# Projection stages with feed-forward parts: the loop over batch elements written out, with normalisations of two elements among the products of the one between

## The chip, the cores and the metric

The kernel runs on one core of a Trainium2 chip. The metric is the device time of one execution in microseconds (us), taken over several executions. TensorE (PE in the rows) multiplies, VectorE is DVE, ScalarE is ACT, GpSimd is POOL, and SyncE (SP) issues nearly all transfers.

## The reference

Two transformer blocks, one behind the other, on x of 4 batch elements x 512 rows x 256 features, with a context of 4 x 1601 x 192. Block 0 has 16 heads of 64, block 1 has 16 heads of 16. Each block does, with `ln` a normalisation over the features:

```python
x = attn(ln(x), ln(x), Wq1, Wk1, Wv1, Wo1, bo1) + x      # self-attention
x = attn(ln(x), context, Wq2, Wk2, Wv2, Wo2, bo2) + x    # cross-attention
x = feed_forward(ln(x)) + x
```

The feed-forward of block 0 is `(a * gelu(gate)) @ Wf` with `a, gate = split(h @ Wp)` (1024 wide each). Block 1 has `gelu(h @ w1) @ w2`, 1024 wide, once between its self- and its cross-attention and once at the end.

## The kernel before

`build` (L1600) runs nine stages one after the other: projections p0, p1, p2, p3, p4 (`project_phase`, L169) and between them attentions a0 to a3. q, k, v and the attention's result o go through DRAM from stage to stage. Every fp32 operand of a large product is split into a high part (fp32r, written by ACT) and a low part (the rest, by DVE), and a product is three products (`product3`, L350): high x high, high x low, low x high. Everything is held feature-major: 128 features on the partitions, 512 rows of x as columns.

A projection stage works through the 4 batch elements. Its steps, as (kind, m), are written out in one list, `order`, which every engine walks through in a hardware loop (`Fori`, L457, L573, L654, L759); the last element is written out once more. The kinds are:

- after 0, after 1 (L505): the attention's output projection of the *next* element, each tile in a PSUM bank of its own (6 and 7); residual (L675): its sum with x_from into x
- mean, var, scale, shift (L513 to L523, L592 to L609, L685 to L716): one normalisation. TensorE forms the mean with a matrix of ones (L499), DVE centres (L689), ACT squares (L595), TensorE forms the variance (L499), DVE adds epsilon (L695) and takes reciprocals (L698), ACT the root into `dev` (L599), DVE scales (L703), ACT writes z_hi (L607) and DVE z_lo (L712). m = 0 is the normalisation ahead of the first products of the next element; m = 1 the one between feed-forward and attention of the present element
- gate 0 to 7 and gate_end (L524, L610, L717): the first feed-forward product, gelu, and the split into u_hi (L588) and u_lo (L670). In p2 a gate has two products (`a` and the gate); in p3 and p4 one
- out 0, out 1 (L535, L733): the second feed-forward product, added to x
- context (L622, L729): the high and the low part of the context, in p1 and p3
- q, k, v (L539, L626, L631, L738): the projections for the next attention. q and k leave as two stores each from a ring of 4 (L402), v as one (L437) from v_sb, which has `VPL` slots: 4 where there is a context and a feed-forward (p3), otherwise 2 (p2)

p2 is projection and geglu feed-forward of block 0 with q, k, v of block 1's self-attention; p3 projection, feed-forward and q, k, v for block 1's cross-attention; p4 projection and feed-forward, whose x is the output. In p2 and p3 the order is such that of the next element only projection, residual and normalisation 0 stand behind the outputs, among q, k and v. In p4 nothing but after 1 stands behind the outputs before the norm.

The order around the change in p2 (L213), and the four DVE banks and one to four ACT banks that it uses (L487 to L494, NAB = 2 in stages with `after`):

```python
order = (gates + [("after", 0)] + outs + [("mean", 1), ("swap_x", 0), ("var", 1), ("after", 1),
                         ("scale", 1), ("shift", 1), ("residual", 0)] + qs[:1] + [("mean", 0)] + qs[1:]
         + ks[:1] + [("var", 0)] + ks[1:] + vs[:2] + [("scale", 0), ("shift", 0)] + vs[2:])
```

Weights come in pieces of up to 128 x 1024 words. Each lands in one of a few rooms (xc, sq, gate and so on, L336), is split (L651, L756; L753 for the lower 64 rows of the context weights), and the whole of them is split before the first residual (L652, L757). x has one buffer, so the store of x (L417) must be read out before the next residual (L679).

Of the kernel before, what the change touches and what calls it, by code (L numbers as in the profile page):

```python
# [16 lines left out]
ALU = mybir.AluOpType  # L17
# [68 lines left out]
def words(ap):  # L86

    return ap.bitcast(F32) if ap.dtype == F32R else ap


class Program:
# [27 lines left out]
    def sem(self, name):  # L119

        handle = self.phase_sems.enter_context(self.nc.semaphore(name))
        self.handles.append(handle)
        return handle
# [45 lines left out]
def project_phase(pr, name, after=None, ff=None, attn=None, x_in=None, x_out=None):  # L169
# [106 lines left out]
    with ExitStack() as st:  # L276
# [382 lines left out]
        def _(dve):  # L659
# [99 lines left out]
            with dve.Fori(0, B - 1, 1) as b:  # L759
                element(b, order)  # L760
            element(B - 1, last_order)


def attend_narrow(pr, name, a):
# [835 lines left out]
def build(nc, ins, out):  # L1600
    with ExitStack() as keep:
        pr = Program(nc, ins, out, keep)
        w0, w1 = "L0_xattn_", "L1_xattn_"
        setup_phase(pr)
        project_phase(pr, "p0", x_in=ins["x"],
                      attn=(SELF0, w0 + "g1", w0 + "b1", w0 + "Wq1", w0 + "Wk1", w0 + "Wv1"))
        attend_wide(pr, "a0", SELF0)
        project_phase(pr, "p1", x_in=ins["x"], x_out=pr.x, after=(SELF0, w0 + "Wo1", w0 + "bo1"),
                      attn=(CROSS0, w0 + "g2", w0 + "b2", w0 + "Wq2", w0 + "Wk2", w0 + "Wv2"))
        attend_wide(pr, "a1", CROSS0)  # L1610
        project_phase(pr, "p2", x_in=pr.x, x_out=pr.x, after=(CROSS0, w0 + "Wo2", w0 + "bo2"),
                      ff=("geglu", w0 + "g3", w0 + "b3", w0 + "Wp", w0 + "bp", w0 + "Wf", w0 + "bf"),
                      attn=(SELF1, w1 + "n1_g", w1 + "n1_b", w1 + "sq_w", w1 + "sk_w", w1 + "sv_w"))
        attend_narrow(pr, "a2", SELF1)
        project_phase(pr, "p3", x_in=pr.x, x_out=pr.x, after=(SELF1, w1 + "so_w", w1 + "so_b"),
                      ff=("gelu", w1 + "n2_g", w1 + "n2_b", w1 + "f1_w1", w1 + "f1_b1", w1 + "f1_w2", w1 + "f1_b2"),
                      attn=(CROSS1, w1 + "n3_g", w1 + "n3_b", w1 + "cq_w", w1 + "ck_w", w1 + "cv_w"))
        attend_narrow(pr, "a3", CROSS1)
        project_phase(pr, "p4", x_in=pr.x, x_out=out, after=(CROSS1, w1 + "co_w", w1 + "co_b"),
                      ff=("gelu", w1 + "n4_g", w1 + "n4_b", w1 + "f2_w1", w1 + "f2_b1", w1 + "f2_w2", w1 + "f2_b2"))  # L1620


# [45 lines left out]
```

## Time and profile before

| | us |
|---|---|
| median of 3 runs | 3775.29 |
| lowest, highest | 3765.72, 3777.51 |
| profiled execution, its own time | 3764.11 |
| span of the profile | 3762.3 |
| mean granted TensorE clock | 0.928 |
| MB moved by the transfers | 588 |
| stage p2: first load issued, last product | 2044.3, 2380.6 |
| stage p3 | 2619.1, 2938.1 |
| stage p4 | 3552.1, 3758.5 |

A busy share is time in which an engine had an instruction under way, over the span. A duration of a TensorE product overlaps the next one, so its pace is read from starts, not from durations. PEclk is the granted TensorE clock as a share of 2.4 GHz. A wait names what ended it, not what caused it. The three stages are 861.8 us of the span when the transfers between their last product and the next stage are left out.

### The profile page before, as it was taken

To read this page: it belongs to the slowest core of one execution; us is meant where nothing else is said; L and a number is where in the kernel's file an instruction comes from. 1 tells how busy PE (TensorE), PEld (TensorE's weight loads), DVE (VectorE), ACT (ScalarE), POOL (GpSimd) and SP (SyncE) were. 2 spreads that over 40 slices of the span, in tenths; PEclk is the share of its full clock that TensorE was granted. 3 is DMA by queue.
4 is the path that set the end of the run, shared out by engine and by line. 5 is a ranking of instruction groups with operands and counts; after the bars stand their busy time and mean duration, and the time that the engine had idled before them with its cause. 6 is when DMAs were issued, how large, how long until landed. Compare 5 with 4: busy or idle time off the path is not lost. (4 is left out here: it accounts for less than half of the span.)

```text
span 3762.3 us, 50843 instructions
## 1 busy us (share of the span) xinstructions
PE 3270.4 (87%) x17084; PEld 1864.8 (50%) x17084; DVE 2258.7 (60%) x4090; ACT 1815.4 (48%) x3349; POOL 1081.9 (29%) x538
## 2 busy tenths in 40 slices
PE   7969995999799999999996778597778599999776
PEld 5734443878544444444443566332566444444254
DVE  4447774334366666666663444496444499999333
ACT  4425552445244444444443333286343188888633
POOL 0036670000077777777775000022000000000000
PEclk9979997999799999999998999698899599999888
DMA  5888866999966666666652331344453523322210
GB/s 204 282 194 225 228 165 244 326 333 302 255 144 148 148 149 148 149 148 148 148 141 103 133 113 39 96 132 147 162 179 102 151 83 106 103 98 88 82 71 34
DMA packets 364807, 588.00 MB, mean 156 GB/s; under 512 B 47042, under 2 KB 200226, under 8 KB 363470
## 3 DMA queue, kind: packets, MB, share of 16 engines
q1 hardware_dynamic: 359478, 582.00, 52.6%
q10 hardware_dynamic: 5112, 3.25, 0.5%
q8 instruction: 118, 1.93, 0.2%
q14 instruction: 99, 0.81, 0.1%
HBM read 341.51 MB, written 240.88 MB: 155 GB/s over the span
## 5 line engine op out<-in xcount | busy, mean ns | idle before, releaser
L1506 ACT ACTIVATE a_prob<-a_ring 128x512 f32<-128x512 f32 (+1 forms) x1088 | 575.4, 601 | 656.3 <-PE a_ring L1411 584.4
L1532 DVE TENSOR_REDUCE a_blk_max<-a_ring 128x1 f32<-128x402 f32 x1024 | 519.5, 567 | 327.6 <-PE a_ring L1395 327.5
L1092 ACT ACTIVATE a_prob<-a_ring 128x512 f32<-128x512 f32 (+1 forms) x1088 | 582.3, 605 | 97.0 <-PE a_ring L1012 93.2
L1361 POOL TENSOR_TENSOR a_prob_sum<-a_prob,a_prob_sum 128x1024 f32<-128x1024 f32 x256 | 599.4, 2379 | 2.7 <-ACT a_prob L1506 2.7
L1137 DVE TENSOR_REDUCE a_blk_max<-a_ring 128x1 f32<-128x402 f32 x1024 | 506.7, 567 | 63.6 <-PE a_ring L999 56.9
L1433 PE MATMUL a_pv<-a_prob,a_v 128*64 128x512 f32 (+1 forms) x2176 | 534.8, 610 | 0.0
L1410 PE MATMUL a_ring<-a_q_stack,a_k_stack 128*128 128x512 f32 (+1 forms) x1088 | 463.9, 426 | 13.8 <-DMA a_q_second<-maxima 12.7
L1411 PE MATMUL a_ring<-a_q_second,a_k_second 65*128 65x512 f32 (+1 forms) x1088 | 435.6, 400 | 0.0
L1361 POOL TENSOR_TENSOR a_prob_sum<-a_prob 128x1024 f32<-128x1024 f32 x128 | 302.0, 2370 | 412.1 <-DVE a_chunk_sum L1563 244.2
L1030 PE MATMUL a_pv<-a_prob,a_v 128*32 128x256 f32 (+2 forms) x4096 | 340.7, 406 | 13.7 <-ACT a_prob L1092 7.8
L742 DVE TENSOR_TENSOR p_split_lo<-p_ps,p_split_hi 128x512 fp32r<-128x512 f32 (+2 forms) x280 | 171.2, 621 | 298.0 <-ACT p_split_hi L630 297.3
L999 PE MATMUL a_ring<-a_k_stack,a_q_stack 63*128 63x402 f32 (+1 forms) x1280 | 284.8, 425 | 65.2 <-DMA a_q_stack<-a_prob 61.1
L1410 PEld LDWEIGHTS a_ring<-a_q_stack,a_k_stack 128*128 128x128 f32 (+1 forms) x1088 | 204.8, 188 | 169.1 <-issue 116.6
L1395 PE MATMUL a_ring<-a_k_stack,a_q_stack 64*128 64x402 f32 (+1 forms) x1280 | 245.5, 428 | 48.0 <-DMA a_q_stack<-q_hi_cross 21.8
L1012 PE MATMUL a_ring<-a_q_stack,a_k_stack 64*128 64x512 f32 (+1 forms) x1088 | 279.8, 484 | 1.0
L630 ACT CAST p_split_hi<-p_ps 128x512 fp32r<-128x512 f32 (+2 forms) x280 | 147.4, 533 | 273.5 <-PE p_ps L355 113.3
L1395 PEld LDWEIGHTS a_ring<-a_k_stack,a_q_stack 64*128 64x128 f32 x1280 | 113.2, 191 | 285.9 <-issue 181.6
L1433 PEld LDWEIGHTS a_pv<-a_prob,a_v 128*64 128x64 f32 (+1 forms) x2176 | 131.7, 137 | 243.8 <-issue 150.8
L999 PEld LDWEIGHTS a_ring<-a_k_stack,a_q_stack 63*128 63x128 f32 x1280 | 146.4, 196 | 164.5 <-issue 68.2
L1411 PEld LDWEIGHTS a_ring<-a_q_second,a_k_second 65*128 65x128 f32 (+1 forms) x1088 | 206.3, 190 | 38.2
L1532 DVE TENSOR_REDUCE a_row_max<-a_ring 128x1 f32<-128x512 f32 x256 | 158.7, 683 | 96.8 <-PE a_ring L1395 96.8
L1012 PEld LDWEIGHTS a_ring<-a_q_stack,a_k_stack 64*128 64x128 f32 (+1 forms) x1088 | 110.7, 182 | 209.9 <-ACT a_prob L1092 81.3
(252 smaller groups left out, 4666.2 us busy)
## 6 DMA issues: line engine op xcount, KB each, us to landing
a_k_stack<-k_hi_cross SPq DMA_DIRECT2D x96, 400.5 KB, 4.6
a_v<-v_cross SPq DMA_DIRECT2D x48, 768.0 KB
a_k_stack<-k_lo_cross SPq DMA_DIRECT2D x80, 400.5 KB, 6.0
a_k_second<-k_hi_cross SPq DMA_DIRECT2D x32, 801.0 KB, 12.7
v_cross<-p_v_sb SPq DMA_DIRECT2D x48, 512.0 KB, 4.1
k_hi_cross<-p_split_hi SPq DMA_DIRECT2D x120, 200.0 KB, 3.2
k_lo_cross<-p_split_lo SPq DMA_DIRECT2D x120, 200.0 KB, 3.2
a_q_stack<-q_hi_self SPq DMA_DIRECT2D x64, 256.0 KB, 4.2
```

The source lines that it names most:

```text
L999: nc.tensor.matmul(ring[:, n % BANKS, 0:a.blk], qst[i % SLOTS][rows, j, t * P:(t + 1) * P], kst[i % SLOTS][rows, j, at:at + a.blk], start= ...
L1012: nc.tensor.matmul(ring[0:keys, n % BANKS, :], kst[i % SLOTS][rows, j, ch * P:ch * P + keys], qst[i % SLOTS][rows, j, :], start=True, stop ...
L1030: last = nc.tensor.matmul(pv[32 * h:32 * h + 32, cols], v[i % SLOTS][0:keys, ch, 32 * h:32 * h + 32], prob[0:keys, tau % RC, h, cols], sta ...
L1092: nc.scalar.activation(prob[0:keys, tau % RC, m, :], ring[0:keys, score_place(e) % BANKS, :], ACT.Exp, scale=a.scale).then_inc(exp_done, 1)
L1137: nc.vector.reduce_max(dst, ring[:, item_place(g) % BANKS, 0:a.blk], AX.X).then_inc(item_read, 1)
L1361: nc.gpsimd.tensor_tensor(prob_sum[:, h], prob_of(i * NCP + cp, h), other, ALU.add)\
L1395: nc.tensor.matmul(ring[:, max_bank(g), 0:a.blk], qst[i % SLOTS][rows, h, t * P:(t + 1) * P], kst[i % SLOTS][rows, h, at:at + a.blk], star ...
L1410: nc.tensor.matmul(out, kst[s][:, h, k0:k0 + keys], qst[s][:, h, :], start=True, stop=False)
L1411: nc.tensor.matmul(out, k2[s][:, h, k0:k0 + keys], q2[s][:, h, :], start=False, stop=True)\
L1433: last = nc.tensor.matmul(pv[64 * h:64 * h + 64, :], v[i % SLOTS][0:keys, ch, 64 * h:64 * h + 64], prob_of(w, h)[0:keys, ch % 2, :], start ...
L1506: nc.scalar.activation(prob_of(w, h)[0:keys, ch % 2, :], ring[0:keys, score_bank(e), :], ACT.Exp, scale=a.scale).then_inc(exp_done, 1)
L1532: nc.vector.reduce_max(dst, ring[:, max_bank(g), 0:a.blk], AX.X).then_inc(item_read, 1)
```

## The change

p2, p3 and p4 are built by a new function, `feed_phase`; `project_phase` stays for p0 and p1. Its instructions are those of `project_phase`, with these differences:

- no hardware loop: one list, `steps`, of (kind, m, element) over all four elements
- x has two buffers, chosen by the element's parity; `dev` is gone and the root goes back into `var`; xc, sq and var stay single
- DVE's tiles use PSUM banks 0 to 3 in turn, projections too, ACT's tiles banks 4 to 7 (NA = 4); each bank's next user waits for the reader of the tile four before
- v_sb has 8 slots in p3 and 4 in p2; the split ring has 3 in p2 and 4 in p3; the second gate buffer of p2 takes as many slots as the first, two
- weights land in 8 rooms of their own that share memory with u; the pieces are split by steps of the list, the later ones after the first residual. The raw context shares memory with its low part, so the context of the next element is loaded once k and v of the present one are done (step load_context); it is split in two halves
- o of element 0 is loaded in chunks of two groups, and its projection starts at the first
- outputs start on the first u_lo tile that is ready; gate steps of p3 and p4 no longer wait for the weights of the second product
- the last x is stored in two halves

```diff
+    def window_plain(b):
+        return (gates(b + 1, 0, 3) + front(b + 2) + gates(b + 1, 3, 4) + norm(0, b + 2, "mean")
+                + gates(b + 1, 4, 6) + norm(0, b + 2, "var") + gates(b + 1, 6, FT) + of(b + 1, outs[:1])
+                + norm(0, b + 2, "scale") + of(b + 1, outs[1:2]) + norm(0, b + 2, "shift") + of(b + 1, outs[2:]))
+
+    def window_self(b):
+        held = of(b - 1, qs + ks) if b == LAST else []
+        held_v = of(b - 1, vs) if b == LAST else []
+        now = b if b != LAST - 1 else B
+        return (gates(b + 1, 0, 1) + norm(1, b, "mean") + gates(b + 1, 1, 4) + held + norm(1, b, "var")
+                + gates(b + 1, 4, 5) + norm(1, b, "scale") + front(b + 2) + held_v + gates(b + 1, 5, 7)
+                + norm(1, b, "shift") + gates(b + 1, 7, FT) + of(b + 1, outs[:1]) + norm(0, b + 2, "mean") + of(now, qs + ks)
+                + norm(0, b + 2, "var") + of(now, vs) + norm(0, b + 2, "scale") + of(b + 1, outs[1:2])
+                + norm(0, b + 2, "shift") + of(b + 1, outs[2:]))
+
+    def window_cross(b):
+        held, now = (b, B) if b == LAST else (B, b if b else B)
+        return (gates(b + 1, 0, 1) + norm(1, b, "mean") + of(b if b else B, [("context", 0)]) + gates(b + 1, 1, 2)
+                + of(b if b else B, [("context", 1)]) + gates(b + 1, 2, 4) + of(held, kvs[:9]) + norm(1, b, "var")
+                + of(held, kvs[9:15]) + gates(b + 1, 4, 6) + norm(1, b, "scale") + of(held, kvs[15:])
+                + front(b + 2) + gates(b + 1, 6, FT) + of(b + 1, outs[:1]) + norm(1, b, "shift")
+                + norm(0, b + 2, "mean") + of(now, kvs[:13]) + norm(0, b + 2, "var")
+                + of(now, kvs[13:]) + of(now + 1, [("load_context", 0)]) + of(b, qs) + norm(0, b + 2, "scale")
+                + of(b + 1, outs[1:2]) + norm(0, b + 2, "shift") + of(b + 1, outs[2:]))
...
+        steps = split(None, w_o) + front(0)
+        if cross:
+            steps += split(w_o, attn[5]) + norm(0, 0, "mean") + of(0, [("context", 0), ("context", 1)])
+            steps += norm(0, 0, "var") + of(0, kvs[:6]) + split(attn[5], w_last) + norm(0, 0, "scale")
+            steps += of(0, kvs[6:12]) + norm(0, 0, "shift") + of(0, kvs[12:]) + of(1, [("load_context", 0)])
+            steps += front(1) + gates(0, 0, 2) + norm(0, 1, "mean") + gates(0, 2, 5) + norm(0, 1, "var")
...
+        elif attn:
+            steps += norm(0, 0, "mean") + split(w_o, w_1) + norm(0, 0, "var") + split(w_1, w_last)
+            steps += norm(0, 0, "scale") + norm(0, 0, "shift") + gates(0, 0, 4) + front(1) + gates(0, 4, 5)
...
+        else:
+            steps += norm(0, 0, "mean") + norm(0, 0, "var") + split(w_o, w_last) + norm(0, 0, "scale")
+            steps += norm(0, 0, "shift") + gates(0, 0, 3) + front(1) + gates(0, 3, 4) + norm(0, 1, "mean")
...
+            def free_d(step):
+                if d_no[step] >= ND:
+                    pe.wait_ge(d_read, d_no[step] - ND + 1)
+                return d_bank(step)
...
+                if kind == "after" and b == 0:
...
+                    pe.wait_ge(w_split, split_by[w_o])
+                    for kt in range(ko):
+                        if kt % OP == 0:
+                            pe.wait_ge(o_first[kt // OP], 32)
...
-        project_phase(pr, "p2", x_in=pr.x, x_out=pr.x, after=(CROSS0, w0 + "Wo2", w0 + "bo2"),
+        feed_phase(pr, "p2", x_in=pr.x, x_out=pr.x, after=(CROSS0, w0 + "Wo2", w0 + "bo2"),
...
-        project_phase(pr, "p3", x_in=pr.x, x_out=pr.x, after=(SELF1, w1 + "so_w", w1 + "so_b"),
+        feed_phase(pr, "p3", x_in=pr.x, x_out=pr.x, after=(SELF1, w1 + "so_w", w1 + "so_b"),
...
-        project_phase(pr, "p4", x_in=pr.x, x_out=out, after=(CROSS1, w1 + "co_w", w1 + "co_b"),
+        feed_phase(pr, "p4", x_in=pr.x, x_out=out, after=(CROSS1, w1 + "co_w", w1 + "co_b"),
```

`front(b)` is after 0, after 1 and residual of element b; a step of an element outside 0 to 3 is nothing; `kvs` are the 8 k and 13 v tiles of p3 mixed in proportion. In both `window` functions with attention the steps of element 2 or 3 that are "held" run in the last window, beside the norm of element 3.

## Rows read from the trace of the kernel before

**Rows 1.** The page, part 1: busy time, share and instructions of each engine.
```profile
PE 3270.4 (87%) x17084; PEld 1864.8 (50%) x17084; DVE 2258.7 (60%) x4090; ACT 1815.4 (48%) x3349; POOL 1081.9 (29%) x538
```

**Rows 2.** Stretches: heads, bodies, one p2 element; engines' busy us, clock, DMA share, GB/s.
```profile
2044.26:2093.62 49.36, 17.75 (x56) 11.54 (x57) 21.66 (x28) 15.09 (x20) 0.69 (x2) 0.67 0.83 293
2093.62:2380.63 287.01, 237.07 (x968) 182.81 (x968) 124.87 (x199) 89.62 (x158) 0.00 (x0) 0.93 0.23 80
2619.11:2663.08 43.97, 14.67 (x33) 8.14 (x33) 18.38 (x27) 12.32 (x19) 1.16 (x2) 0.62 0.67 234
2663.08:2938.13 275.05, 223.70 (x980) 173.88 (x980) 127.53 (x195) 119.83 (x223) 0.00 (x0) 0.95 0.48 153
3552.10:3587.83 35.73, 12.32 (x32) 7.27 (x33) 16.17 (x22) 11.31 (x15) 0.00 (x0) 0.64 0.62 221
3587.83:3758.51 170.68, 131.24 (x480) 96.51 (x480) 57.19 (x90) 57.69 (x95) 0.00 (x0) 0.86 0.11 40
2169.22:2244.16 74.94, 61.40 (x256) 47.34 (x256) 33.70 (x54) 23.49 (x42) 0.00 (x0) 0.96 0.32 112
```

**Rows 3.** Waits of PE, 2093.62 to 2380.63 (p2): us in total, times, longest.
```profile
PE p_ps L355 <- ACT p_v_sb L644: 20.9, 3, 8.2
PE p_ps L355 <- DVE p_z_lo L712: 14.3, 4, 7.7
```

**Rows 4.** The same view, 2663.08 to 2938.13 (p3).
```profile
PE p_ps L355 <- DVE p_z_lo L712: 19.1, 5, 7.7
PE p_ps L368 <- ACT p_v_sb L644: 13.9, 10, 3.1
PE p_ps L355 <- ACT p_gate L616: 13.1, 10, 1.7
```

**Rows 5.** The same view, 3587.83 to 3758.51 (p4).
```profile
PE p_ps L355 <- DVE p_z_lo L712: 23.3, 3, 8.0
...
PE p_ps L499 <- ACT p_sq L595: 6.5, 3, 2.2
```

**Rows 6.** Timeline of PE in p2: start, duration, instruction.
```profile
2098.15 0.40 PE L355 MATMUL p_ps<-p_z_hi,p_L_xattn_Wp_hi 128*128 128x512 f32 x1
...
2116.97 0.39 PE L355 MATMUL p_ps<-p_z_hi,p_L_xattn_Wp_lo 128*128 128x512 f32 x1
...
2155.98 1.88 PE L499 MATMUL p_ps<-p_sq,mean_ones 128*128 128x512 f32 x4
...
2157.93 0.40 PE L355 MATMUL p_ps<-p_z_lo,p_L_xattn_sk_w_hi 128*128 128x512 f32 x1
```

**Rows 7.** Stretches as in rows 2: 490 us of attention a1; 3 us behind a gap.
```profile
1500.00:1990.00 490.00, 490.00 (x2194) 234.39 (x2191) 336.10 (x639) 230.38 (x438) 363.73 (x157) 1.00 0.60 143
3634.00:3637.00 3.00, 3.00 (x7) 2.42 (x8) 0.00 (x0) 0.29 (x2) 0.00 (x0) 0.50 0.00 0
```

**Rows 8.** Timeline of ACT at the end of p2.
```profile
2382.93 0.37 ACT L644 COPY p_v_sb<-p_ps 128x256 f32<-128x256 f32 x1 [3.39 <-DMA v_self<-p_v_sb]
```

**Rows 9.** Timeline of ACT in p3: table load, first gelu, context.
```profile
2737.73 1.28 ACT L616 ACT_TABLE_LOAD   x1 [1.81 <-PE p_ps L355]
2739.02 0.69 ACT L616 ACTIVATE p_gate<-p_ps,vectors 128x512 f32<-128x512 f32 x1
2739.61 2.86 ACT L625 CAST p_c_hi<-p_ctx_raw 128x3204 fp32r<-128x3204 f32 x1
```

**Rows 10.** Timeline of DVE: low part of the context (p3), of a weight piece (p2).
```profile
2812.58 3.50 DVE L731 TENSOR_TENSOR p_c_lo<-p_ctx_raw,p_c_hi 128x3204 fp32r<-128x3204 f32 x1 [8.89 <-ACT p_c_hi L625]
...
2050.54 1.23 DVE L756 TENSOR_TENSOR p_L_xattn_Wo_lo<-p_xc,p_L_xattn_Wo_hi 128x1024 fp32r<-128x1024 f32 x1 [9.85 <-ACT p_L_xattn_Wo_hi L651]
```

**Rows 11.** Stretch at the start of p2: DMA share, GB/s at the end.
```profile
2044.00:2063.00 19.00, 0.00 (x0) 0.00 (x0) 2.45 (x2) 2.09 (x2) 0.69 (x2) 0.50 0.95 331
```

**Rows 12.** The v stores at L437: ns min/median/max of an issue.
```profile
L437 SPq DMA_DIRECT2D v_cross<-p_v_sb x104: 340/383/1933, 664.7 to 2938.6; - x104
```

**Rows 13.** Stretch of one p3 element, columns as in rows 2.
```profile
2736.00:2806.00 70.00, 56.81 (x253) 43.42 (x253) 34.45 (x53) 30.86 (x58) 0.00 (x0) 0.98 0.54 173
```

461 lines of the change are left out of this document (added).

## The prediction

> **What bounds the kernel now.** I read the page first, then stretches, waits and spacings of the three stages that the change touches (p2, p3, p4). The page: TensorE is busy 87% of the span [rows 1]. No other engine is near, so what matters is where TensorE stands still or runs at its lower clock. The profiled execution took 3764.1 us, 11 under the median of the runs (3775.3).
>
> Each stage is cut in a **head** (first load issued to first gate product) and a **body** (to the last product) [rows 2]. Heads: 49.4, 44.0, 35.7 us; bodies: 287.0, 275.1, 170.7 us. Together 861.8 us. What the change can win lies there; the attention stages (p0, a0, p1 and so on) are compiled from the same lines.
>
> The waits of TensorE in the bodies tell what it stands still for. p2: 20.9 us in three waits put down to the copy into v_sb, 14.3 for z_lo (the end of a normalisation) [rows 3]. p3: 19.1 for z_lo, 13.9 for v_sb, 13.1 for the gelu that frees a bank [rows 4]. p4: 23.3 for z_lo in three waits (the fourth element's is put down otherwise) and 6.5 for squares, 2.2 the longest [rows 5]. So each element pays a normalisation, about 7.7 us after its variance and 2.2 before it, because too little independent work is queued behind the statistic.
>
> The second loss is the clock. A 512-column product follows the last after 18.82/83 = 0.227 us (83 steps lie between the first two rows), and a statistic holds TensorE 1.72 us (1.95 to the product after next, less one product) [rows 6]. Behind a gap of 7.7 us, stretch 3634 to 3637 shows the clock at 0.50: the 1.2 GHz level, 7 products in 3 us. In 490 us without a gap it is 1.00, 2.4 GHz [rows 7]. The bodies stand at 0.93, 0.95 and 0.86 [rows 2].
>
> **The change, part by part.** No product is added or removed. The loop over elements is written out, x has two buffers, and normalisation of element b+2 (feed-forward) and b (attention) stands among the gate and output products of b+1.
>
> Full-clock product time of the bodies. Gates and outputs: p2 96+48 products, q and k 24, v 24 of half width counted as 12: 180 x 0.227 = 40.9 an element, four times 163.5; projections of three later elements 3 x 48 x 0.227 = 32.7; 14 statistics 24.1. **p2: 220.** p3: gates and outputs 96 and q 12 an element, 24.5, times four 98; k and v of three elements (element 0's now stand in the head): 8 x 5 of 402 columns at 0.178 (0.227 by width) and 13 x 5 at 0.118 (half width and a little), 15 each, 45; projections of two elements 10.9; 14 statistics 24.1. **p3: 178.** p4: 96 an element, 87; three projections 16.3; 6 statistics 10.3. **p4: 114.** An element of p2 takes 74.9 us now [rows 2]; its work is 58.9.
>
> Cover of the moved norms. After var come the addition, two reciprocals, root, scale and shift, in all the 7.7 us. In p4 two gates (2.7) and both outputs (10.9) stand behind it, in p2 v and both outputs (13.9): hidden. Before var stand two gates (2.7) for 2.2 us of squares: hidden, barely. DVE has 33.7 and ACT 23.5 us of work per 74.9 us element [rows 2], and they fit into 58.9. If the cover fails, it is because DVE, in order, holds u_lo behind the reciprocals; the three gate buffers allow for that once. The separate bank pools (four for DVE's tiles, four for ACT's) take away most of the 13.1 us for gelu.
>
> v_sb: four slots instead of two in p2, eight instead of four in p3. That is most of 20.9 and 13.9, and at the end of p2 ACT's copy waited 3.4 us for a store that a fourth slot makes unnecessary [rows 8]; the next stage starts 3.4 earlier.
>
> ACT tables: roots now stand between gates, so p2 and p3 switch four times an element instead of two. A load is 1.28 us, and the gelu starts 0.01 behind its end [rows 9]: 2.6 us more for ACT, hidden. The Trainium skill (ScalarE: Activation LUTs, "What ACT_TABLE_LOAD costs") counts a drain of about 1.38 us with every switch, which speaks against this change; the row does not show it. By the page eight switches on exposed chains (heads, last windows) would add 11 us, 3605.
>
> What stays open in the bodies. **p2:** 1.6 us lower clock at the start (8 products at 0.2 extra), 0.9 for the last output, then the last element's attention norm: 7.7 less 3.0 of held v products, 4.7; 1.6 of lower clock after it; 5 for small waits: 14, **234**. **p3:** window 0 has no k or v products (element 0's went to the head), so the squares stand open, 2.2. The last window needs its context split first (2.9 on ACT [rows 9], 3.5 on DVE [rows 10], now in two halves): with squares before it 6.6, and 4 around it. In two windows context parts sit before gates in both queues: 6 together. Stores: an element's k and v are 6.5 MB (16 stores of 128 x 400 and 13 of 128 x 512 words) in 15 us of products, 420 GB/s, against 331 reached at a share of 0.95 [rows 11]. Slots hold 3.7 MB, so most of it drains later, but the projection inputs and context now share that time: bound 0 to 7 an element; I take 3.5 for three, 11. Sum 30, **208**. Context loads, formerly an element ahead, wait now until the products have read it, because it shares room with c_lo; 1.6 MB at 331 GB/s and 2 of latency, 7 us, have 16 us of cover. **p4:** 1.6 and 2: **117**.
>
> Heads. Weights, formerly all split before the first residual, are now split between steps, and element 0's projection starts on the first chunk of o. p2: the last of 5.5 MB lands after 19.4 us (17.4 at 331 GB/s and 2 for latency); 12 products instead of 48 remain, 22.5. Then the chain, 16: residual 1.5 (two passes of half a 1.23 us piece [rows 10], rounded up for PSUM), mean 1.9, squares 2.2, var 2.9 at the low clock, 7.7: 38.7. Four pieces before var delay it 2.5, five behind the reciprocals stand in DVE's way with 2 x 1.23 and three half-size, 4.5: **46**, for 49.4. Where those pieces were covered before, by the DMA wait, they now cost. p4: 14.2 to 16.5 for the projection, 16 of chain, 4.9 for four pieces: **36.6**, for 35.7. p3: 17 for the projection, 16 of chain, context 3.5 and a little, pieces 5.6, low parts of k between; k tiles five on wait for a DVE that still splits weights; then the rest of k and v and 5.4 of projection 1: **52.4**, but 20.8 of it was in the body before.
>
> Sum: 46 + 234 + 52.4 + 208 + 36.6 + 117 = 694 against 861.8; with the 3.4 a saving of 171. On the execution's own 3764 that gives 3593; the runs lie 1 to 13 us above it, and I set the number between, **3600**.
>
> SP's queue issues in the order of steps: each load stands directly behind the step that frees its buffer, and the 29 stores of an element's k and v at 0.38 us an issue [rows 12] take 11 of the 15 us in which they are made. Nothing later of TensorE's order is ahead of anything earlier there.
>
> **Rivals.**
> B, the covers leak: in-order ACT and DVE and the store bandwidth take back much. Each of some eleven windows loses 4 us (a reciprocal before u_lo, a late square), p3's k and v run at DMA speed (22 for 15, four times, 28): 72 lost, 3665. For it: 420 against 331 GB/s; p3's present gelu waits of up to 1.7 behind a context split. Against: four banks each.
> C, slower: the clock does not stay up. The new stream is broken into groups by many waits below 1 us; if each let the clock fall, the 512 us of body products would stretch. It decides at a granted clock of 0.75 (512/0.75 is 171 more), and at 0.70 the time is 3764 - 171 + 220 = 3813. Against it: 490 us of attention stream at 1.00 [rows 7] and 0.98 in a p3 stretch of 70 us with several short waits [rows 13]. The Trainium skill (TensorE: Matmul & The Clock Gate, "A second HAM failure mode: psum-queue depth-cycling") reports a kernel whose clock swung because it paused between groups while cycling banks; by that rule C happens; those rows contradict it.
> D, it does not do what it says: engines still meet at each norm, since the statistic needs the newest x. Nothing but v_sb slots and banks is won against longer heads: within 10 us of 3764. Against it: the steps are written with two elements between product and norm.
> E, everything is hidden, also stores and context: 30 us more, 3570.
>
> **How the numbers follow.** Forecast 0.66, B 0.22, E 0.06, C 0.04, D 0.02. The range, 3570 to 3660, takes in E and nearly B; the price bounds of the stores (0 to 28) and of head pieces (0 to 15) lie within. A measurement can tell about 0.3%, 11 us, from no change. Faster 0.94, same 0.02, slower 0.04.
>
> **What would show it.** Right: bodies of about 234, 208, 117 us at a clock of 0.97 or more; z_lo waits gone but for one or two per stage; v_sb waits gone in p2; heads no shorter than 36 us. B shows as TensorE waiting for p_gate, p_split or v_sb in p3 beside a DMA share near 0.9. C shows as a clock under 0.9 in a body. Wrong altogether if a body keeps four z_lo waits, or if a store's landing ends most of p3's waits.

## The result, and the profile after

The kernel with the change takes **3598.3 us** (median of 4 runs, 3595.4 to 3605.6), against 3771.5 (4 runs, 3765.7 to 3777.5) for the kernel before in the same comparison: a ratio of 0.9547, 95% interval 0.9529 to 0.9566. The profiled execution spans 3596.5 us against 3762.3.

First the page, part 1; it answers to [rows 1]:

```profile
PE 3231.5 (90%) x17084; PEld 1855.9 (52%) x17084; DVE 2256.9 (63%) x4094; ACT 1825.5 (51%) x3365; POOL 1082.9 (30%) x538
```

TensorE runs the same 17084 products and is busy 39 us less; the other 127 us of the span's 166 were idle time. In the bodies of p2 and p4 the granted clock rose (rows below and [rows 2]), so fewer products ran at the low one. ACT has 16 instructions more: 12 table loads and the second halves of four context splits.

Then the stretches, head and body of p2, p3 and p4, columns as in [rows 2]:

```profile
2045.70:2092.05 46.35, 19.11 (x56) 12.51 (x57) 21.15 (x28) 15.44 (x21) 1.17 (x2) 0.65 0.87 311
2092.05:2324.32 232.27, 225.74 (x968) 178.07 (x968) 123.86 (x199) 94.28 (x165) 0.00 (x0) 0.98 0.28 99
2562.35:2616.28 53.93, 36.35 (x161) 30.47 (x162) 26.62 (x38) 23.51 (x43) 2.12 (x2) 0.80 0.83 283
2616.28:2824.08 207.80, 187.47 (x852) 150.17 (x850) 118.67 (x187) 115.91 (x209) 0.00 (x0) 0.95 0.55 176
3440.41:3476.60 36.19, 12.27 (x32) 7.70 (x33) 15.84 (x22) 10.94 (x15) 0.00 (x0) 0.69 0.62 218
3476.60:3593.33 116.73, 116.73 (x480) 91.83 (x480) 56.20 (x90) 56.73 (x95) 0.00 (x0) 0.98 0.17 61
```

| us | before | forecast | after |
|---|---|---|---|
| p2 head, body | 49.4, 287.0 | 46, 234 | 46.4, 232.3 |
| p3 head, body | 44.0, 275.1 | 52.4, 208 | 53.9, 207.8 |
| p4 head, body | 35.7, 170.7 | 36.6, 117 | 36.2, 116.7 |
| sum | 861.8 | 694 | 693.3 |

The gain lies in the bodies. p4's body holds no gap at all: TensorE is busy all 116.73 us. What TensorE still waits for in the bodies of p2 (first two rows) and p3 (the rest), by the waits of PE, which answers to [rows 3, 4]; columns: us in total, times, longest. A view of [rows 3, 4 and 5] counts one z_lo wait that belongs to the head, since it ends with the body's first product; so does that of p2 here, and it is left out (14.0 us).

```profile
PE p_ps L977 <- issue: 5.7, 1, 5.7
PE p_ps L1086 <- DVE p_x L1317: 0.8, 1, 0.8
...
PE p_ps L989 <- issue: 8.4, 1, 8.4
PE p_ps L1086 <- ACT p_sq L1184: 4.6, 1, 4.6
PE p_ps L977 <- issue: 3.1, 1, 3.1
PE p_ps L989 <- ACT p_gate L1213: 1.8, 2, 1.5
PE p_ps L989 <- ACT p_v_sb L1236: 1.1, 1, 1.1
```

In `feed_phase` L977 is `product3`, L989 the context product, L1086 a statistic. Before, [rows 3, 4] give 35.2 us for v_sb and z_lo in p2 and 46.1 for z_lo, v_sb and gelu in p3; less the 7.7 of each head these are 27.5 and 38.4 in the bodies. Now p2 has one wait of weight, 5.7 us, for the z of its last attention normalisation, and p3 has 20.2 us with the two waits under 1 us that are left out here. "issue" means that the view names no releaser; the engines' timelines are needed.

Outside the three stages nothing was won: 3762.3 less 861.8 is 2900.5 us, 3596.5 less 693.3 is 2903.2.

### The profile page after: what moved, and what is told of

Same layout as the page of the kernel before. It is cut to its first block and busy times, and to the rows that moved or that the text cites. A ratio compares the mean times of both kernels' runs of the same rounds, so it can differ in the third digit from the quotient of the medians.

```text
span 3596.5 us, 49786 instructions
## 1 busy us (share of the span) xinstructions
PE 3231.5 (90%) x17084; PEld 1855.9 (52%) x17084; DVE 2256.9 (63%) x4094; ACT 1825.5 (51%) x3365; POOL 1082.9 (30%) x538
## 5 line engine op out<-in xcount | busy, mean ns | idle before, releaser
L742 DVE TENSOR_TENSOR p_split_lo<-p_ps,p_split_hi 128x402 fp32r<-128x402 f32 (+1 forms) x224 | 137.7, 623 | 263.6 <-ACT p_split_hi L630 260.2
L1957 PE MATMUL a_ring<-a_k_stack,a_q_stack 64*128 64x402 f32 (+1 forms) x1280 | 246.1, 428 | 51.1 <-DMA a_q_stack<-q_hi_cross 23.3
L630 ACT CAST p_split_hi<-p_ps 128x402 fp32r<-128x402 f32 (+1 forms) x224 | 119.0, 535 | 214.2 <-PE p_ps L355 84.6
```

The source lines that it names most:

```text
L1957: nc.tensor.matmul(ring[:, max_bank(g), 0:a.blk], qst[i % SLOTS][rows, h, t * P:(t + 1) * P], kst[i % SLOTS][rows, h, at:at + a.blk], star ...
```

## The experiments

All kernels are the changed kernel with one edit, x10 to x12 with two to four, and x13 goes back to the old function in two stages. "Sum" is the three stages, from first load to last product, of the profiled execution: 693.3 us in the changed kernel. A stage that an edit does not touch came out up to 2.3 us different from run to run, and the interval of a ratio is about 6 to 9 us to either side, so small effects are read from their own stretch.

**Old order, all else new** (`x9_old_order_all`). For each element b the list is written as it was before, with after 0 and 1 together behind the variance; p3 likewise, with element 0's k and v back behind its outputs:

```diff
...
+            steps += gates(b, 0, 3) + of(b if b and cross else B, [("context", 0), ("context", 1)]) + gates(b, 3, FT)
+            steps += of(b, outs[:3])
+            if not attn:
+                steps += of(b, outs[3:]) + front(b + 1)
+                for part in ("mean", "var", "scale", "shift"):
+                    steps += norm(0, b + 1, part)
+            elif not cross:
+                steps += norm(1, b, "mean") + of(b, outs[3:]) + norm(1, b, "var") + front(b + 1)[:2]
+                steps += norm(1, b, "scale") + norm(1, b, "shift") + front(b + 1)[2:] + of(b, qs[:1])
+                steps += norm(0, b + 1, "mean") + of(b, qs[1:] + ks[:1]) + norm(0, b + 1, "var") + of(b, ks[1:] + vs[:2])
+                steps += norm(0, b + 1, "scale") + norm(0, b + 1, "shift") + of(b, vs[2:])
...
```

> All three stages unrolled, with two x buffers, four and four banks and the new slots, but the steps in the old order: both normalisations of an element stand behind its own outputs. Theory (it is the order that hides the normalisations): per element the squares (2.2 us) and the 7.7 us after the variance are open again where fewer products stand behind them, with the lower clock behind each. p4 three times 9.9 and some clock, +42; p2 about +20, since the 20.9 us for v_sb stay won; p3 about +30. Sum +92, 3690 us. Rival (unrolling, banks and slots gave the time, the order little): 3598 to 3610. Rival (the order gave all of it): 3760 or more.

Measured: 3719.4 us (ratio to before 0.9873, 0.9857 to 0.989), 121 above the changed kernel. Its stretches, columns as above:

```profile
2045.83:2092.19 46.36, 19.12 (x56) 12.56 (x57) 21.14 (x28) 15.44 (x21) 1.17 (x2) 0.65 0.87 311
2092.19:2371.46 279.27, 233.76 (x968) 181.63 (x968) 125.63 (x199) 87.70 (x159) 0.00 (x0) 0.93 0.23 82
2608.80:2647.87 39.07, 11.71 (x32) 7.29 (x33) 21.61 (x29) 15.83 (x22) 2.12 (x2) 0.67 0.72 264
2647.87:2899.56 251.69, 216.20 (x980) 171.86 (x980) 124.00 (x197) 115.77 (x224) 0.00 (x0) 0.94 0.49 162
3520.76:3555.15 34.39, 11.81 (x32) 7.01 (x33) 15.84 (x22) 10.94 (x15) 0.00 (x0) 0.65 0.63 229
3555.15:3715.94 160.79, 128.84 (x480) 96.52 (x480) 57.48 (x90) 57.69 (x95) 0.00 (x0) 0.87 0.12 45
```

With all else new, the order is worth 118 us of the 168 (sum 811.6), between the expectation of the theory (92) and that of "all of it" (160): 47 in p2, 29 in p3 (head and body), 42 in p4, where 20, 30 and 42 were expected. But the 118 are not all open normalisations. ACT and PE in p2, then ACT in p3:

```profile
2162.42 0.59 ACT L1257 CAST p_split_hi<-p_ps 128x512 fp32r<-128x512 f32 x1 [11.06 <-DMA q_lo_self<-p_split_lo]
...
2163.43 0.74 ACT L1218 ACTIVATE p_var<-p_var 128x256 f32<-128x256 f32 x2
...
2167.62 0.77 PE L1007 MATMUL p_ps<-p_z_hi,p_L_xattn_Wp_hi 128*128 128x512 f32 x1 [10.90 <-DVE p_z_lo L1325]
...
2720.13 2.95 ACT L1251 CAST p_c_hi<-p_ctx_raw 128x1602 fp32r<-128x1602 f32 x2 [6.15 <-DMA p_ctx_raw<-ctx_in]
```

In two windows of p2 ACT waits 11 us for the landing of a q store before it can split the fourth of the element's q and k tiles: the ring has three slots in the new function and had four. The root of the normalisation (L1218) stands behind that split, and TensorE waits 10.9 us each time. In the third window no store is in the way, and the wait is 4.0 us. The two extra waits are twice 6.9, 13.8 us. In p3 ACT waits 6.2, 6.9 and 5.6 us for the context's load, which now has to wait for room, and TensorE stands 16.9 us behind it, in three waits for p_gate. The kernel before shows neither. So some 31 us of the 118 arise only where the old order meets the new ring and the new context room; by difference about 88 are left for the order alone (33, 12 and 42 in the three stages). No run separates them.

**Two v_sb slots in p2** (`x2_p2_two_v_slots`):

```diff
-    VPL = 8 if cross else 4
+    VPL = 8 if cross else 2
```

> p2 with two v_sb slots as before, instead of four. Theory of the prediction (the 20.9 us of v_sb waits in p2 were for slots): the waits come back in good part, p2's body +10 us (5 to 20), 3608 us. Rival (those waits were normalisations held up in ACT's queue, since all v copies stand in one place and a store lands in 2 to 3 us): p2's body within 4 us, 3598 to 3602, at most the stage's end 3 us later.

Measured: 3597.2 us (3596.4 to 3600.2). Waits of PE in p2's body:

```profile
PE p_ps L977 <- issue: 8.5, 1, 8.5
```

No wait for v_sb; the one wait for the last normalisation grows from 5.7 (the same in every kernel with four slots and four banks) to 8.5, and the body from 232.3 to 235.3. In the new order two slots cost 3 us, as the rival said. That does not yet say what the 20.9 us of [rows 3] were in the old order. The trace of the kernel before does; DVE, ACT and PE in p2, the first of the three waits:

```profile
2164.37 1.68 DVE L712 SCALAR_TENSOR_TENSOR p_z_lo<-p_sq,vectors,p_z_hi 128x256 fp32r<-128x256 f32 x4 [0.26 <-ACT p_z_hi L607]
...
2167.98 0.37 ACT L644 COPY p_v_sb<-p_ps 128x256 f32<-128x256 f32 x1 [2.85 <-DMA v_self<-p_v_sb]
...
2169.22 0.80 PE L355 MATMUL p_ps<-p_z_hi,p_L_xattn_Wp_hi 128*128 128x512 f32 x1 [7.09 <-ACT p_v_sb L644]
```

z_lo was ready at 2166.05, but the gate product also needs a bank that the last copies into v_sb free, and those waited 2.85 us for the landing of a v store. So 3.2 of this wait's 7.1 us were for slots (and banks), and by the same reading 4.2 and 1.7 of the other two (z_lo ready at 2239.93 and 2316.37, products at 2244.16 and 2318.11): 9.1 of the 20.9. The other 11.8 were the normalisation. It fits that x9, with four slots in the old order, shows 4.0 us in its undisturbed window, where 7.1, 8.2 and 5.7 stood before.

p3's first load came 238.7 us behind the last product with two slots and 238.0 with four, so the end of the stage and the attention behind it gained nothing either.

**Two banks for ACT's tiles** (`x3_two_act_banks`):

```diff
-    ND, NA = 4, 4
+    ND, NA = 4, 2
```

> Two instead of four PSUM banks for ACT's tiles in all three stages. Theory: TensorE meets gelu more often, short waits under 1.5 us as the 13.1 us of gelu waits of before; p3 +8, p4 +3, p2 +2, together +13, 3611 us, and the granted clock in the bodies stays at 0.95 or above. Rival C (a stream broken by many short waits loses its clock): bodies below 0.90, over 3650 us. Rival (banks cover nothing that the three gate buffers do not): 3598.

Measured: 3607.1 us (3600.1 to 3614.4), +8.8. Bodies of p2 and p3:

```profile
2092.47:2329.76 237.29, 228.62 (x968) 180.02 (x968) 123.84 (x199) 94.54 (x165) 0.00 (x0) 0.97 0.28 97
2622.09:2833.35 211.26, 187.01 (x852) 149.25 (x850) 118.78 (x187) 117.29 (x209) 0.00 (x0) 0.97 0.52 167
```

p2 +5.0, p3 +3.5; p4 at 116.5 is unchanged. The clock does not fall: 0.97 in p2 and p3, 0.98 in p4. The second pair of banks is worth some 8 us, much less than the order.

**Half the slots in p3** (`x4_p3_half_slots`):

```diff
-    SPL = 4 if cross else 3
-    VPL = 8 if cross else 4
+    SPL = 2 if cross else 3
+    VPL = 4
```

> p3 with two split slots and four v_sb slots instead of four and eight. Theory: the k and v stores of an element (6.5 MB) cannot be made in the 15 us of its products, slots take up the difference; with half of them TensorE waits for landings three to four times, p3's body +15 us (8 to 25), 3613 us. Rival (stores drain as fast as the products are made, slots are not needed): within 4 us, 3598 to 3602. Rival B (store speed limits already with all slots): +25 or more, since each slot missing is waited for in full.

Measured: 3609.4 us (3606.0 to 3612.7), +11.1. Stretch of p3's body, then its waits:

```profile
2620.60:2838.07 217.47, 188.34 (x852) 149.38 (x850) 118.68 (x188) 115.71 (x210) 0.00 (x0) 0.95 0.52 167
```

```profile
PE p_ps L977 <- issue: 8.3, 2, 7.1
PE p_ps L1136 <- issue: 2.8, 2, 2.1
```

The body is 9.7 us longer: 5.2 more at L977, and 2.8 at L1136, where the changed kernel has no wait. ACT now waits 28.3 us for the landing of k stores before it splits, in 18 waits; with all slots it is 13.0 in 6. So the slots of p3 do take up stores. The edit halves both rings at once, and their shares are not separated.

**Pieces earlier** (`x5_pieces_earlier`), in p2 alike:

```diff
-            steps += norm(0, 0, "mean") + norm(0, 0, "var") + split(w_o, w_last) + norm(0, 0, "scale")
+            w = split(w_o, w_last)
+            steps = steps[:-1] + w[:2] + steps[-1:] + w[2:3] + norm(0, 0, "mean") + w[3:]
+            steps += norm(0, 0, "var") + norm(0, 0, "scale")
```

> Two weight pieces are split before the first residual and one before the first mean in p2 and p4, so that fewer stand in the chain of the first normalisation. Theory (pieces in DVE's order hold up the chain, 4.6 us in p4 between reciprocal and scale): heads of p2 and p4 each 3 to 4.5 us shorter, 3591 us. Rival (the raw weights land too late to be split there, or the first residual now waits for them): heads unchanged or up to 3 us longer.

Measured: 3585.2 us (3582.7 to 3586.6). The heads of p2 and p4 are 43.2 and 32.8 us, 3.2 and 3.4 shorter. DVE in p4's head, first the changed kernel, then this one; columns: start, duration:

```profile
3465.17 3.36 DVE L1282 RECIPROCAL p_var<-p_var 128x256 f32<-128x256 f32 x2
3468.45 4.56 DVE L1257 TENSOR_TENSOR p_L_xattn_f_w_lo<-p_w_raw,p_L_xattn_f_w_hi 128x1024 fp32r<-128x1024 f32 x4
3472.93 1.67 DVE L1287 SCALAR_TENSOR_TENSOR p_sq<-p_xc,vectors,p_var 128x256 f32<-128x256 f32 x4
```

```profile
3457.68 3.37 DVE L1285 RECIPROCAL p_var<-p_var 128x256 f32<-128x256 f32 x2
3460.97 1.57 DVE L1290 SCALAR_TENSOR_TENSOR p_sq<-p_xc,vectors,p_var 128x256 f32<-128x256 f32 x4
```

The 4.56 us between reciprocal and scale are gone. p4's gain is clear: with this edit the head is 31.5 to 32.9 us in three kernels, without it 35.3 to 36.8 in the others with the new order. p2's is less so: 43.2, 44.5 and 44.8 with the edit, 44.5 to 47.1 without. The two heads make up 6.6 of the 13 us of the median; p3's stretch, which the edit doesn't touch, was 2.2 shorter in the same profile, and the rest is not explained by it.

**q ahead of the variance in p3's first window** (`x6_q_before_var`):

```diff
-                + norm(0, b + 2, "mean") + of(now, kvs[:13]) + norm(0, b + 2, "var")
-                + of(now, kvs[13:]) + of(now + 1, [("load_context", 0)]) + of(b, qs) + norm(0, b + 2, "scale")
+                + norm(0, b + 2, "mean") + of(now, kvs[:13]) + of(b if not b else B, qs) + norm(0, b + 2, "var")
+                + of(now, kvs[13:]) + of(now + 1, [("load_context", 0)]) + of(b if b else B, qs) + norm(0, b + 2, "scale")
```

> In the first window of p3 the q products stand between mean and variance instead of behind the variance. Theory (nothing covers the squares there, since element 0's k and v are in the head: 4.6 us and the lower clock behind them): gap gone, 4.5 to 6 us, 3593 us. Rival (the squares stand behind z_hi and copies in ACT's order, and later work is then uncovered): the gap moves behind the variance, 3598.

Measured: 3591.6 us (3588.0 to 3598.0); p3's body:

```profile
2615.67:2818.94 203.27, 185.14 (x852) 149.10 (x850) 118.62 (x187) 115.81 (x209) 0.00 (x0) 0.97 0.56 179
```

4.5 us shorter. The wait for the squares is gone from the list, and a smaller one at L977 is new ("issue: 5.8, 2, 3.1" for "3.1, 1, 3.1"): 4.6 taken away, 2.7 come back, and the clock rises from 0.95 to 0.97. The head in front of it was 0.9 us shorter here too, so that much can be noise.

**The gap of 8.4 us in p3's last window** took three runs. In the changed kernel SP, ACT, DVE and PE there read (from a timeline of each):

```profile
2782.56 0.38 SPq L1003 DMA_DIRECT2D p_ctx_raw<-ctx_in  x1
...
2789.11 1.29 ACT L1184 ACTIVATE p_sq<-p_xc 128x512 f32<-128x512 f32 x2 [8.90 <-DVE p_xc L1273]
2791.51 2.96 ACT L1221 CAST p_c_hi<-p_ctx_raw 128x1602 fp32r<-128x1602 f32 x2 [1.10 <-DMA p_ctx_raw<-ctx_in]
...
2793.07 3.57 DVE L1314 TENSOR_TENSOR p_c_lo<-p_ctx_raw,p_c_hi 128x1602 fp32r<-128x1602 f32 x2 [3.32 <-ACT p_c_hi L1221]
...
2796.73 0.55 PE L989 MATMUL p_ps<-p_L_xattn_cv_w_hi,p_c_hi 128*128 128x256 f32 x1 [8.44 <-issue]
```

The products that free the context's room ended at 2771.8, the load is issued at 2782.6, lands at 2791.5, and c_lo is ready at 2796.6. The first explanation was that SP comes to the load too late.

Issue the v stores from POOL (`x7_v_stores_pool`):

```diff
-                elif kind == "v":
+                elif kind == "v" and not cross:
...
+            for step in steps if cross else []:
+                kind, m, b = step
+                if kind == "v":
+                    pool.wait_ge(a_read, a_no[step] + 1)
...
+                    pool.dma_start(dst.rearrange("g p m -> p g m"),
...
```

> The v stores of p3 are issued from POOL's queue instead of SP's. Theory (SP's queue is behind: its issues of k and v stores take 0.55 to 1.06 us each and it comes to the load of the last context 11 us after the products that free it): the load starts 8 us earlier, the 8.4 us gap of the last window falls to about 2, 3591 us. Rival (the stores' bytes, not their issues, hold the load): gap stays, 3598. Rival (POOL issues slower and v_sb slots come free later): new waits for v_sb, 3600 to 3605.

Or only the context's loads (`x8_context_pool`):

```diff
-                elif kind == "load_context":
-                    sp.wait_ge(d_tile, ctx_last[b - 1] + 1)
-                    sp.wait_ge(a_tile, v_last[b - 1] + 1)
-                    load_context(b)
...
+            for kind, m, b in steps if cross else []:
+                if kind == "load_context":
+                    pool.wait_ge(d_tile, ctx_last[b - 1] + 1)
+                    pool.wait_ge(a_tile, v_last[b - 1] + 1)
+                    pool.dma_start(ctx_raw[:], pr.ins["ctx"][b]).then_inc(ctx_later, 16)
```

> Only the loads of contexts 1 to 3 are issued from POOL's queue, the stores stay on SP's. Theory of SP's queue: the same 6 us as with the v stores moved, as the load no longer stands behind stores, 3591 us. Rival (bytes): the load is issued early but lands no earlier, because it shares the engines with the stores still under way, 3598.

Measured: 3604.3 us (3598.7 to 3607.3) and 3600.4 (3592.6 to 3604.6); p3's body 214.7 and 211.2, so 6.9 and 3.4 longer; the gap 7.2 in both. With the v stores on POOL, 0.75 us each there, SP's own issues grew, and the context load went out 19.4 us behind the first k store of the element, against 20.0. The time is that of the rival with new waits for v_sb, but those waits did not grow (1.1 us, as before), so its reason is not shown. With only the loads on POOL the load went out at once, 0.6 us behind the end of the last product that reads the context, but (POOL, then ACT, of `x8_context_pool`):

```profile
2781.79 0.53 POOL L1072 DMA_DIRECT2D p_ctx_raw<-ctx_in  x1 [53.21 <-PE p_ps L990]
...
2790.89 0.59 ACT L1229 CAST p_split_hi<-p_ps 128x512 fp32r<-128x512 f32 x1 [7.10 <-DMA k_lo_cross<-p_split_lo]
...
2799.10 1.29 ACT L1186 ACTIVATE p_sq<-p_xc 128x512 f32<-128x512 f32 x2 [4.97 <-DVE p_xc L1275]
2800.30 2.94 ACT L1223 CAST p_c_hi<-p_ctx_raw 128x1602 fp32r<-128x1602 f32 x2
```

The context landed 8.9 us after its issue, at 2790.7, and nothing took it up for ten microseconds: in ACT's order its split stands behind the squares of the last element, which need the last output. The k stores land later instead, and ACT waits 7.10 us for one. The wait at L977 is also 4.2 us longer, so the body is longer and not shorter. So two things stand in series, and the gap falls only when both go. That is `x10_last_context_early`: the last load alone on POOL, and the split ahead of the centring:

```diff
-        return (gates(b + 1, 0, 1) + norm(1, b, "mean") + of(b if b else B, [("context", 0)]) + gates(b + 1, 1, 2)
-                + of(b if b else B, [("context", 1)]) + gates(b + 1, 2, 4) + of(held, kvs[:9]) + norm(1, b, "var")
+        early, late = (b, B) if b == LAST else (B, b if b else B)
+        return (gates(b + 1, 0, 1) + of(early, [("context", 0), ("context", 1)]) + norm(1, b, "mean")
+                + of(late, [("context", 0)]) + gates(b + 1, 1, 2) + of(late, [("context", 1)]) + gates(b + 1, 2, 4) + of(held, kvs[:9]) + norm(1, b, "var")
...
+            if cross:
+                pool.wait_ge(d_tile, ctx_last[LAST - 1] + 1)
+                pool.wait_ge(a_tile, v_last[LAST - 1] + 1)
+                pool.dma_start(ctx_raw[:], pr.ins["ctx"][LAST]).then_inc(ctx_later, 16)
```

> Only the load of the last context is issued from POOL's queue, and the last context is split ahead of the last element's centring and squares in ACT's and DVE's order. Theory (the gap of 7 to 8 us in p3's last window is made of two things in series, a load behind SP's stores and a split behind the squares; taking away the load alone left 7.2 us): gap down to 1 or 2 us and less low clock behind it, p3's body 8 us shorter, 3590 us. Rival (the load that comes earlier holds up k stores, ACT waits for their landing and the split starts no sooner): gap 5 us or more, 3597.

Measured: **3586.1 us** (3579.4 to 3588.0). p3's body, then ACT and DVE:

```profile
2616.30:2815.06 198.76, 185.01 (x852) 147.68 (x850) 118.39 (x187) 115.53 (x209) 0.72 (x1) 0.97 0.57 185
```

```profile
2783.66 2.96 ACT L1227 CAST p_c_hi<-p_ctx_raw 128x1602 fp32r<-128x1602 f32 x2
...
2785.79 3.56 DVE L1320 TENSOR_TENSOR p_c_lo<-p_ctx_raw,p_c_hi 128x1602 fp32r<-128x1602 f32 x2
```

The gap is 1.5 us and the body 9.0 shorter. That both have to go is supported by this run and x8; the split moved ahead with the load left on SP was not tried.

**Together** (`x11_pieces_and_q`: the edits of x5 and x6; `x12_all_three`: with x10 as well).

> The earlier weight pieces (heads of p2 and p4) and the q products ahead of the variance (p3) together. They lie in different stages, so they should add: 3598 less 6 for the heads less 6 for the squares, 3584 to 3586 by what the traces of each alone showed in their stages, 3579 if the medians of each alone are right. Rival (they share something): above 3590.

> All three edits together: 8 us below the two without the early last context, 3571 to 3577 us. Rival (the early load costs what it gives): as the two alone, 3580 to 3586.

Measured: 3588.7 us (3576.9 to 3591.5; sum 685.6) and **3576.4 us** (3575.2 to 3579.1; ratio to before 0.9484, 0.9468 to 0.9499; sum 674.4). The two edits without x10 lie between what was expected (3584 to 3586) and the rival (above 3590), with runs 15 us apart. Their sum of stages is 7.7 us below the changed kernel's, but x5 alone came to 684.9 and to a lower median, so these runs don't show that the q products add anything to the earlier pieces. The three together are as expected, p3's body 195.7 at a clock of 0.98, and faster than the kernel before and the changed kernel.

**Only p4 new** (`x13_only_p4_new`, `project_phase` for p2 and p3):

```diff
-        feed_phase(pr, "p2", ...
+        project_phase(pr, "p2", ...
-        feed_phase(pr, "p3", ...
+        project_phase(pr, "p3", ...
```

> p4 alone is built by the new function, p2 and p3 as before. Theory (each stage wins by itself): p4's body 116 us instead of 170.7, head 36, everything else as before: 53 us below the kernel before, 3717 us. Rival (part of the gain is a state that one stage leaves to another, clock or queue): differs from 53 by over 8 us.

Measured: 3711.7 us (3707.8 to 3722.7), 59 below before (interval of the ratio 0.9826 to 0.9873, 48 to 66 us). In the trace p4's head and body are 36.7 and 115.9, 53.8 less than before: p4 wins what it wins without the other two. The same was not tried for p2 and p3. Built as before, those two came out 6.6 longer and 3.0 shorter than in the profile of before, so an untouched stage can also differ by more than 2.3.

## Why the prediction was right, step by step

**The sum.** 694 us for three stages, 693.3 measured. No stretch is off by more than 1.7 us. The terms inside are less exact than that, and the agreement is in part luck. The profiled execution was forecast at 3593 and took 3598.3: the 3.4 us at the end of p2 did not come, and the rest of the span grew by 2.7. The 3600 lies nearer to the median than that, because 7 us were added for runs slower than the profiled one; now the profiled execution stands in the middle of the runs.

**Full-clock product time and cover.** Right. p4 was set at 114 + 3 and is 116.7 with no gap: both gates and both outputs hide all that stands behind and before the variance. x9 shows that it is the order that does it: in p4, where nothing else gets in the way, 42 us, as expected.

**The reading of the z_lo waits.** One wait in each of [rows 3, 4, 5], 7.7, 7.7 and 8.0 us, is the head's. "p4: 23.3 for z_lo in three waits (the fourth element's is put down otherwise)" is therefore two waits of the body, 15.3 us, and one of 7.7 put down otherwise: three normalisations in the body. No term of the sum used the 23.3, so nothing followed from it.

**"v_sb: four slots instead of two in p2, eight instead of four in p3. That is most of 20.9 and 13.9."** Too large. In the old order 9.1 of the 20.9 us in p2 were for slots and the banks behind them, 11.8 were the normalisation, and in the new order two slots instead of four cost 3 us (x2). The body's total came out right because the order removed both parts. In p3 the slots matter: halving split and v_sb slots together costs 10 us (x4), and how much of the 13.9 they won is not shown.

**"The separate bank pools take away most of the 13.1 us for gelu."** Two banks instead of four cost 3.5 us in p3 and 5.0 in p2, with 5.6 us of waits for p_gate in p3 instead of 1.8. With four banks and the old order (x9) the ten short waits of [rows 4] are gone as well; the 16.9 us for p_gate that p3 shows there are three waits behind the late context. So the pools do take most of the 13.1 away, and the order takes most of it too.

**At the end of p2, 3.4 us.** Failed. The next stage's first load comes 5.5 us after the last product (before 6.4), but a2's first product waits 28.70 us after p2's last, before 28.87, so only 0.2 us were won:

```profile
2353.02 3.60 PE L1561 MATMUL a_ring<-a_k_stack,a_q_stack 63*128 63x512 f32 x10 [28.70 <-DMA a_q_stack<-a_prob]
```

What ended last there is a chain of small transfers that ACT's queue issues, not ACT's copy. The prediction took a wait on an engine and didn't follow it to the next stage's first product.

**p2, open 14.** Measured 12.3 (232.3 less 220): 5.7 for the last attention normalisation (4.7 forecast), 0.8 for the last output, and by difference 5.8 of low clock, where 3.2 were set (1.6 twice). The 5 us for small waits are not there, so two wrong terms nearly cancel. p4 shows why 1.6 is too little: behind its head twelve products, not eight, follow each other in 0.44 us on average instead of 0.23, which costs 2.5 us.

**p3, open 30.** Measured 29.8 (207.8 less 178), where 30 was forecast, but of other parts, so the agreement is luck: the gaps are 20.2, and the rest, 9.6, is put down to the clock at 0.95. Squares of window 0: 4.6 for 2.2, because the z of the attention normalisation stands ahead of them, z_hi on ACT (1.71 us) and z_lo on DVE (1.68), where the centring comes behind it. Last window: 8.4 and low clock, for 10.6. Context parts ahead of gates: 2.9 (gate and v_sb waits) for 6. Stores: 11 forecast; no gap of that kind shows on TensorE. They show elsewhere: the 29 issues of element 2 take SP 21 us instead of 11, ACT waits up to 3.9 us for a slot, and the context load goes out late. That was the step "the 29 stores at 0.38 us an issue take 11 of the 15 us": the 0.38 is the median of v stores in p1 and p3 [rows 12], and these issues take 0.66 us on average. Not forecast: 3.1 for the last z.

**Heads.** p2 46.4 and p4 36.2 as worked out, with the pieces in the chain as the price (2.5 and 4.5 us set in p2, 4.9 in p4): x5 takes 3.2 and 3.4 of it back. p3 is 1.5 longer than forecast.

**Rival B** (leaks of 4 us in every window, k and v at store speed): no. No wait of TensorE for a landing shows among p3's k and v, and the eleven windows lose about 4 us or more in three places (5.7, 4.6 and 8.4), not in each. **C** (clock): no. The bodies stand at 0.98, 0.95 and 0.98; before they were at 0.93, 0.95 and 0.86. p3's 0.95 has not risen and lies under the 0.97 that the prediction named as a sign of being right. x3, with half the banks, leaves 0.97 in p2 and p3. In this kernel the low clock (1.2 GHz) shows behind gaps of microseconds. A statistic takes 1.98 us behind a gap of 0.84, and twice that behind 4.6:

```profile
2667.93 3.78 PE L1086 MATMUL p_ps<-p_sq,mean_ones 128*128 128x512 f32 x4 [4.59 <-ACT p_sq L1184]
```

The Trainium skill (TensorE: Matmul & The Clock Gate, "A second HAM failure mode: psum-queue depth-cycling") reports a clock that swings with short pauses between groups while banks are cycled; these bodies cycle banks and do not show that. **D** (it doesn't do what it says): no; x9, with the normalisations put back, loses 118 us. **E** (everything hidden, 3570): no; it took three more edits to come to 3576.

**Table loads.** With roots between gates the whole kernel has 22 loads ahead of a root and 18 ahead of a gelu, formerly 16 and 12. ACT in p3, a timeline:

```profile
2654.71 1.28 ACT L1188 ACT_TABLE_LOAD   x1
2656.00 0.73 ACT L1188 ACTIVATE p_var<-p_var 128x256 f32<-128x256 f32 x2
2656.75 1.28 ACT L1213 ACT_TABLE_LOAD   x1
```

The root starts 0.01 us behind the load, and the next load 0.02 behind the root. The Trainium skill (ScalarE: Activation LUTs, "What ACT_TABLE_LOAD costs") counts a drain of about 1.38 us with every switch; none shows here, so the estimate of 3605 by that page has nothing to stand on, though 3605 and 3598 alone could hardly be told apart by the time.

**Open.** The 50 us between the kernel before and x9 are not broken up, and they are net of the 31 us of waits that x9 has for q stores and the context: banks (8) and p3's slots (10) were tried in the new order only, the early start on o, the split of weights between steps and the doubled x were not tried alone. x9 with a ring of four in p2 was not tried either.

## What to carry to other kernels

If the engine that bounds the kernel stands still for a chain of small operations on other engines, put one more element between the chain's start and its use: here that gave about 88 to 118 of 168 us, while more buffers and banks gave about 8 to 10 each in the new order, and 3 in one stage. A wait that a profile puts down to a copy says which event came last. Look what that copy itself waited for, and when the other inputs were ready: here a wait of 7.1 us was 3.9 of normalisation and 3.2 of a store's landing. Halving a buffer in the new kernel tells what it is worth there, not what it cost before. And an experiment that puts one part of a change back may bring waits that neither kernel has; read its own waits before you take its whole loss for the worth of that part. Where moving one blocker leaves a gap as long as it was, look for a second one in series in another engine's order before giving up the first.

## What was not expected of the hardware

SP needed longer to issue a transfer where more transfers were under way. One line, L1010, issues k_hi and k_lo in p2, where the DMA share is 0.28, and in p3, where it is 0.55 over the body and 1.00 (299 GB/s) from 2762 to 2783 us, around element 2's k and v stores. The view of that line in the changed kernel; columns: ns min/median/max of an issue, first and last start:

```profile
L1010 SPq DMA_DIRECT2D k_hi_cross<-p_split_hi x32: 319/680/1261, 2594.3 to 2821.5; - x32
...
L1010 SPq DMA_DIRECT2D k_hi_self<-p_split_hi x8: 319/320/555, 2185.8 to 2322.9; - x8
```

The least time is the same, the median about twice as long in p3, for tiles that are no larger (200 KB against 256). That the load is the cause is not shown by itself, but it fits x7: with the v stores on POOL's queue, SP's issues in the same stretch reached 1.83 us, and k stores landed 7.9 and 8.8 us after issue (k_hi and k_lo, medians) instead of 3.4 and 3.3. The second queue did not relieve the first: while that element's k and v were stored, 282 GB/s were moved, against 304 with all stores on SP.
